# Layer 0's squared interactions as four tiles of 128 rows, two of 117 and a stacked half tile, in place of seven tiles of 117

## The reference

```python
z = einsum('bhd,bkd,hks->bsd', x0, xk, W) + b[None, :, None]
z = relu(z)
# layers 0 and 1: the first 64 maps are the next layer's xk, the other 64 go to the output
# layer 2: all 128 maps go to the output
```

## Time and profile before

| | |
|---|---|
| median of the runs | 2503.74 us (3 runs, 2494.42 to 2505.49) |
| the profiled execution | 2490.02 us, its span 2488.2 us |
| granted TensorE clock, mean over the span | 0.996 |
| PE, DVE, POOL, ACT busy | 96%, 90%, 67%, 43% |
| q1, the queue of the large DMAs | 461.35 MB, busy 76.7% of 16 engines |

### The profile page before, as it was taken

The page is one execution under the profiler, slowest core; times in us unless marked ns, Lnnn a source line. Parts: engine busy times, 40 slices in busy tenths (PEclk is TensorE's granted clock), DMA queues, the critical chain, the costliest instruction groups (busy, mean ns, idle before and its releaser), DMA issues. The chain is left out here.

```text
span 2488.2 us, 29429 instructions
## 1 busy us (share of the span) xinstructions
PE 2399.6 (96%) x7702; PEld 1442.7 (58%) x7702; DVE 2240.9 (90%) x1657; ACT 1058.4 (43%) x1053; POOL 1679.1 (67%) x1059
## 2 busy tenths in 40 slices
PE   0899999999999999999999999999999999999989
PEld 0465555665565666556556655656665555665556
DVE  0799998999999999999999999999999998999993
ACT  0244443444444444444444444443444443444445
POOL 7877766767677676777767677776768767544340
PEclk9999999999999999999999999999999999999999
DMA  6888787998778789888779887888988777888730
GB/s 162 203 197 196 193 191 183 208 215 191 190 199 191 196 212 213 189 190 199 191 196 216 207 190 187 201 192 197 215 210 188 192 197 173 210 205 195 182 79 11
DMA packets 172546, 469.79 MB, mean 189 GB/s; under 512 B 28987, under 2 KB 63163, under 8 KB 172245
## 3 DMA queue, kind: packets, MB, share of 16 engines
q1 hardware_dynamic: 148869, 461.35, 76.7%
q0 software_dynamic: 19968, 5.15, 2.2%
q10 hardware_dynamic: 3680, 2.95, 0.5%
HBM read 457.02 MB, written 12.33 MB: 189 GB/s over the span
## 5 line engine op out<-in xcount | busy, mean ns | idle before, releaser
L638 POOL TENSOR_TENSOR low<-prod,high 128x1024 fp32r<-128x1024 f32 x384 | 945.9, 2473 | 553.7 <-ACT high L801 551.2
L914 DVE TENSOR_TENSOR prod<-spread,maps 128x2048 f32<-128x2048 f32 x448 | 1016.7, 2281 | 72.8 <-ACT direct L743 20.9
L801 ACT ACTIVATE high<-prod 128x1024 fp32r<-128x1024 f32 (+1 forms) x576 | 596.2, 1056 | 715.9 <-DVE prod L914 458.4
L616 POOL DMA_INDIRECT landed<-in_tbl,rows_id x585 | 620.6, 1061 | 165.6 <-issue 148.6
L1014 PE MATMUL zacc_a<-prod,w_plain 128*128 128x512 f32 (+1 forms) x1536 | 709.1, 596 | 17.0 <-DVE prod L899 11.1
L1014 PE MATMUL zacc_b<-prod,w_plain 128*128 128x512 f32 (+1 forms) x1536 | 706.2, 594 | 5.9 <-DVE prod L914 5.9
L1014 PEld LDWEIGHTS zacc_a<-prod,w_plain 128*128 128x128 f32 (+1 forms) x1536 | 291.9, 190 | 288.9 <-issue 259.9
L1014 PEld LDWEIGHTS zacc_b<-prod,w_plain 128*128 128x128 f32 (+1 forms) x1536 | 291.2, 190 | 275.0 <-issue 246.8
L899 DVE TENSOR_TENSOR prod<-shifted,x_thrice 117x1024 f32<-117x1024 f32 x224 | 266.7, 1230 | 66.8 <-DMA shifted<-x_periods 53.7
L1049 PE MATMUL zacc_b<-low,w_high 128*128 128x512 f32 x672 | 281.2, 499 | 6.2 <-POOL low L638 6.2
L1049 PE MATMUL zacc_a<-low,w_high 128*128 128x512 f32 x672 | 280.7, 498 | 0.7 <-DVE low L869 0.5
(11 more groups left out here) (103 smaller groups left out, 1618.9 us busy)
## 6 DMA issues: line engine op xcount, KB each, us to landing
spread<-x_periods SPq DMA_DIRECT2D x608, 512.0 KB, 16.5
shifted<-x_periods SPq DMA_DIRECT2D x188, 468.0 KB
x_thrice<-x_periods SPq DMA_DIRECT2D x93, 156.0 KB
shifted<-x_periods SPq DMA_DIRECT2D x64, 156.0 KB
landed<-in_tbl,rows_id POOLq DMA_INDIRECT x585, 4.6
spread<-x_periods SPq DMA_DIRECT2D x32, 256.0 KB, 20.7
x_periods<-x SPq DMA_DIRECT2D x30, 256.0 KB, 2.2
spread<-features SPq DMA_DIRECT2D x4, 512.0 KB, 4.6
```

The lines of the kernel that those rows point to most:

```text
L616: nc.gpsimd.indirect_dma_start(out=landed[:, f, :], out_offset=None, in_=tables[f], in_offset=bass.IndirectOffsetOnAxis(ap=rows[:, f:f + 1 ...
L638: nc.gpsimd.tensor_tensor(low[0:rows, at_, :], prod[0:rows, at_, :], high[0:rows, slot(j, SPLIT, NH), :], ALU.subtract).then_inc(s_lowp, 1)
L801: nc.scalar.activation(high[0:rows, h, :], made(turn, j)[0:rows, :], ACT.Copy).then_inc(s_round, 1)
L914: nc.vector.tensor_tensor(prod[:, at_:at_ + 2, :], spread[:, t:t + 2, :], maps[:, :].unsqueeze(1).to_broadcast([128, 2, COLS]), ALU.mult). ...
```

## The change

Layer 0's 780 products are laid out anew. Tiles u = 0 to 3 get 11 more rows (117 to 127): fields 0 to 10 with the shifts 19, 18, 20, 21 (SPARE_SHIFTS). What is left for tile u = 6 is 40 rows (LAST_ROWS), which fit in half a tile: it becomes a stacked V tile of 64 rows. Its first operand is not x_thrice but a new buffer x_last. The weights are laid out to match (host side, laid_out).

- Each of u = 0 to 3 gets a second load of 11 rows (44 KB); x_thrice gets a fourth load of 11 rows; u = 6 is loaded by two DMAs of 20 rows (80 KB) in place of two of 39 rows, and x_last by two more of 20 rows, at the end of load_first. That makes 7 more DMAs a turn on SP's queue.
- Tile 26 is V: ACT makes its high part, DVE its low part (after the product of tiles 29 and 30), PE contracts it with four fp32r matmuls at tile 28 in place of four fp32 instructions at tile 26. At tile 26 PE does nothing; the count of s_mm for it is added at tile 25 (silent).
- ACT's take of layer 0 waits for PE's tile 28 and moves from tile 29 to tile 30 of its list.
- In the prologue load_thrice0 and load_shifted0 issue the extra rows too (one DMA with part 0, four with part 1), and load_last follows them. DVE clears half of x_last once.

```diff
+assert SHIFTS == PER0 * (N0 - 1) + 2
+SPARE = ROWS - TRIPLE
+SPARE_SHIFTS = (19, 18, 20, 21)
+LAST_RUN, LAST_GAPS = 10, ((19, 11, 20), (18, 11, 21))
+LAST_ROWS = 4 * LAST_RUN
...
-PLAN = "FVFPPPFPFFDPFDVFFPFV" "FFFFFFF" "FPFFFVPFDPVFDPPDFPFV"
+PLAN = "FVFPPPFPFFDPFDVFFPFV" "FFFFFFV" "FPFFFVPFDPVFDPPDFPFV"
-RELU0_AT, RELU1_AT, RELU2_AT = N1 + N0 - 1 + 3, N1 - 1 + 2, 3
+RELU0_AT, RELU1_AT, RELU2_AT = N1 + N0 - 1 + 4, N1 - 1 + 2, 3
...
 def rows_of(j):
     if j in SQUARED:
-        return TRIPLE
+        return HALF if j == SQUARED[-1] else ROWS if j - N1 < len(SPARE_SHIFTS) else TRIPLE
     t = j if j in PAIRED else j - N1 - N0
     return HALF * min(2, FIELDS - 2 * t)
-def shifts_of(u):
-
-    return min(PER0, SHIFTS - PER0 * u)
+def loads_of(u):
+
+    return 4 if u == N0 - 1 else 2 if u < len(SPARE_SHIFTS) else 1
+
+
+def last_pairs():
+
+    taken = {min((r, (r + e) % FIELDS), ((r + e) % FIELDS, r)) for r in range(SPARE) for e in SPARE_SHIFTS}
+    for n, (shift, first, gap) in enumerate(LAST_GAPS):
+        for t in range(LAST_RUN):
+            for b in range(2):
+                f = first + gap * b + t
+                g = (f + shift) % FIELDS
+                once = f < FIELDS and min((f, g), (g, f)) not in taken
+                yield 2 * LAST_RUN * n + 2 * t + b, f % FIELDS, g, once
 def stacked(j):
...
-                nc.sbuf_tensor("x_thrice_r", [TRIPLE, COLS], f32r) as x_thrice_r:
+                nc.sbuf_tensor("x_thrice_r", [ROWS, COLS], f32r) as x_thrice_r:
-        shifted = sb("shifted", [TRIPLE, RING0, COLS])
-        x_thrice = sb("x_thrice", [TRIPLE, COLS])
+        shifted = sb("shifted", [ROWS, RING0, COLS])
+        x_thrice = sb("x_thrice", [ROWS, COLS])
+        x_last = sb("x_last", [HALF, COLS])
...
         def load_thrice0(engine, part):
+            if part == 0:
+                engine.dma_start(x_thrice[TRIPLE:ROWS, :], chunk0(0, SPARE)).then_inc(s_thrice, 16)
             for s in range(PER0):
                 for lo, hi in runs_of(FIELDS - s, part):
                     engine.dma_start(x_thrice[s + PER0 * lo:s + PER0 * (hi - 1) + 1:PER0, :], chunk0(FIELDS - s + lo, hi - lo)
...
         def load_shifted0(engine, u, part):
+            if part == 1:
+                engine.dma_start(shifted[TRIPLE:ROWS, u, :], chunk0(SPARE_SHIFTS[u], SPARE)).then_inc(s_shifted[u], 16)
             for lo, hi in runs_of(PER0 * u, part):
                 engine.dma_start(shifted[PER0 * lo:PER0 * hi, u, :], chunk0(PER0 * u + lo, hi - lo).unsqueeze(1)
                                  .to_broadcast([hi - lo, PER0, COLS])).then_inc(s_shifted[u], 16)
...
+            def load_last(n, to, second):
+
+                for i, (shift, first, gap) in enumerate(LAST_GAPS):
+                    rows = period(n, first + (shift if second else 0), 2 * gap).rearrange("(b t) c -> t b c", b=2)
+                    sp.dma_start(to[2 * LAST_RUN * i:2 * LAST_RUN * (i + 1), :], rows[0:LAST_RUN, :, :]
+                                 ).then_inc(s_shifted[N0 - 1], 16)
+
             def load_shifted(n, u):
-                if shifts_of(u) == PER0:
-                    sp.dma_start(shifted[:, u % RING0, :], period(n, PER0 * u, FIELDS).unsqueeze(1).to_broadcast(
-                        [FIELDS, PER0, COLS])).then_inc(s_shifted[u], 16)
+                if u == N0 - 1:
+                    load_last(n, shifted[:, u % RING0, :], True)
                     return
-                for s in range(shifts_of(u)):
-                    sp.dma_start(shifted[s:TRIPLE - PER0 + s + 1:PER0, u % RING0, :], period(n, PER0 * u, FIELDS)
+                sp.dma_start(shifted[0:TRIPLE, u % RING0, :], period(n, PER0 * u, FIELDS).unsqueeze(1).to_broadcast(
+                    [FIELDS, PER0, COLS])).then_inc(s_shifted[u], 16)
+                if u < len(SPARE_SHIFTS):
+                    sp.dma_start(shifted[TRIPLE:ROWS, u % RING0, :], period(n, SPARE_SHIFTS[u], SPARE)
                                  ).then_inc(s_shifted[u], 16)
             def load_first(n):
...
                 for s in range(PER0):
                     sp.dma_start(x_thrice[s:TRIPLE - PER0 + s + 1:PER0, :], period(n, FIELDS - s, FIELDS)
                                  ).then_inc(s_thrice, 16)
+                sp.dma_start(x_thrice[TRIPLE:ROWS, :], period(n, 0, SPARE)).then_inc(s_thrice, 16)
                 for u in range(RING0):
                     load_shifted(n, u)
+                load_last(n, x_last, False)
             def load_spread(n, q):
                 for h in range(2):
...
+            sp.wait_ge(s_zero, 1)
+            load_last(Turn(None, 0), x_last, False)
...
+            nc.vector.memset(x_last[HALF // 2:HALF, :], 0.0).then_inc(s_zero, 1)
...
                     if u == 0 and turn.fixed and turn.number() == -1:
                         dve.wait_ge(s_prep, 3 if PARTED0 else 2)
                     if u == 0:
-                        dve.wait_ge(s_thrice, nxt.count(16 * PER0, 16 * PER0 + EXTRA_THRICE))
-                    loads = 1 if shifts_of(u) == PER0 else shifts_of(u)
+                        dve.wait_ge(s_thrice, nxt.count(16 * PER0 + 16, 16 * PER0 + 16 + EXTRA_THRICE))
+                    loads = loads_of(u)
                     dve.wait_ge(s_shifted[u], nxt.count(16 * loads, 16 * loads + EXTRA_SHIFTED[u]))
-                    nc.vector.tensor_tensor(to, shifted[0:rows, u % RING0, :], x_thrice[0:rows, :],
+                    nc.vector.tensor_tensor(to, shifted[0:rows, u % RING0, :], (x_last if u == N0 - 1 else x_thrice)[0:rows, :],
                                             ALU.mult).then_inc(s_square, 1)
                     return
                 t = j if j in PAIRED else j - N1 - N0
...
+            def silent(j):
+
+                return j < TILES and stacked(j) and PLAN[j - LATE] not in SPLIT
+
...
                     then = step_back(turn, j, LATE)
                     if then and PLAN[then[1]] in SPLIT:
                         done = contract_low(*then)
-                    done.then_inc(s_mm, 1)
+                    if not silent(j):
+                        done.then_inc(s_mm, 2 if silent(j + 1) else 1)
                 if turn.fixed and (turn.number(), j) in (
                         (-1, SQUARED[-1]), (CHUNKS - 1, PAIRED[-1]), (CHUNKS - 1, TILES - 1)):
```

More of the change, by code:

```diff
@@ L247, in build @@
         x = sb("x", [128, TURNED, ROWS])
-        with nc.sbuf_tensor("shifted_r", [TRIPLE, RING0, COLS], f32r) as shifted_r, \
-                nc.sbuf_tensor("x_thrice_r", [TRIPLE, COLS], f32r) as x_thrice_r:
-            pass
-        shifted = sb("shifted", [TRIPLE, RING0, COLS])
-        x_thrice = sb("x_thrice", [TRIPLE, COLS])
+        with nc.sbuf_tensor("shifted_r", [ROWS, RING0, COLS], f32r) as shifted_r, \
+                nc.sbuf_tensor("x_thrice_r", [ROWS, COLS], f32r) as x_thrice_r:
+            pass
+        shifted = sb("shifted", [ROWS, RING0, COLS])
+        x_thrice = sb("x_thrice", [ROWS, COLS])
+        x_last = sb("x_last", [HALF, COLS])
         direct01 = sb("direct01", [128, COLS])
@@ L286, in build @@
         s_thrice = sem("s_thrice")
+        s_zero = sem("s_zero")
         s_shifted = [sem(f"s_shifted{u}") for u in range(N0)]
@@ L709, in _ @@
                 act.wait_ge(s_prep, 1)
-                nc.scalar.activation(w_high[0:TRIPLE, parts12:plan_r, :], parts_in[0:TRIPLE, parts12:plan_r, :], ACT.Copy
+                nc.scalar.activation(w_high[:, parts12:plan_r, :], parts_in[:, parts12:plan_r, :], ACT.Copy
                                      ).then_inc(s_cast, 1)
@@ L852, in _ @@
             if PARTED0:
-                squares = parts_in[0:TRIPLE, parts12:plan_r, :]
+                squares = parts_in[:, parts12:plan_r, :]
                 done = nc.vector.tensor_tensor(squares, squares, w0_other[:, PLAIN0:N0, :], ALU.add)
@@ L860, in _ @@
                 dve.wait_ge(s_cast, 2)
[L861 to L862 removed]
+                nc.vector.tensor_tensor(w_low[:, parts12:plan_r, :], parts_in[:, parts12:plan_r, :],
+                                        w_high[:, parts12:plan_r, :], ALU.subtract).then_inc(s_prep, 1)
             def low_part(turn, j):
@@ L1164, in tile @@
         return np.concatenate([rows, rows]) if stacked(j) else rows
-    ab, ba = np.zeros((TRIPLE, N0, MAPS), np.float32), np.zeros((TRIPLE, N0, MAPS), np.float32)
+    ab, ba = np.zeros((ROWS, N0, MAPS), np.float32), np.zeros((ROWS, N0, MAPS), np.float32)
     for n, j in enumerate(SQUARED_ORDER):
         u, i = j - N1, np.arange(FIELDS)
-        for s in range(shifts_of(u)):
+        if u == N0 - 1:
+            for row, f, g, once in last_pairs():
+                if once:
+                    ab[row::HALF, n], ba[row::HALF, n] = w0[f, g], w0[g, f]
+            continue
+        for s in range(PER0):
             f, g = (i - s) % FIELDS, (i + PER0 * u) % FIELDS
-            ab[s::PER0, n] = w0[f, g]
+            ab[s:TRIPLE:PER0, n] = w0[f, g]
             if (u, s) != (0, 0):
-                ba[s::PER0, n] = w0[g, f]
+                ba[s:TRIPLE:PER0, n] = w0[g, f]
```

(4 more changed lines are left out.)

10 lines of the change are left out of this document (4 added, 6 removed).

## The result

The kernel after takes **2535.56 us** (median of 4 runs, 2532.56 to 2538.02) against 2503.70 for the kernel before (4 runs): ratio 1.013, 95% interval 1.0109 to 1.0151, or 31.9 us more. The forecast was 2515, 10.7 us of working on top of before. The sign and the place are as forecast; the size is three times as large. Of the signs that the forecast named, two turns take 146.65 us and not 145.6, and PE's busy time is 14.7 us less and not 24 us.

The account below looks back on a forecast made before the run. PE was taken to set the pace at 72.7 us a turn. New wait 3.7, late turns 4.3 and prologue 2.7 gave +10.7 us on the 2503.7 median, 2514.4, rounded to 2515 us; range 2496 to 2540.

Parts of the forecast that it names:

- the signs that the forecast named: Checks in the profile, among them two turns about 145.6 us apart and PE's busy time down some 24 us.
- PE's part: Tile 26 on PE: 0.78 us a turn less, 24 us over 31 turns if nothing waits; 128 rows cost nothing.
- The new wait: PE idles 0.8 us for tile 26's low part from DVE; tile 29 starts 0.12 us later, +3.7 us in all.
- Late turns: Late product of tile 27, formerly hidden, now delays PE: 1.9 us in turns 2 to 30, 2.4 in the last, +4.3.
- DVE's list: One more DVE instruction, 1.13 us a turn, absorbed by its waits for PE after tile 30: costed at nothing.
- The tight 0.7 us of ACT's tile 32: ACT's high part of tile 32 ready at S + 20.2, wanted by PE at S + 20.9: tight, costs nothing.
- Prologue: Before the turns: extra small loads on SP 1.6 us, plus layer 0's end at 4.2 us for 3.1; together +2.7 us.
- The sum: Whole kernel: 3.7 + 4.3 + 2.7 = +10.7 us, carried over to the median, 2515 us.
- The first: Rival, chance 0.15: tile 26's low part comes before PE wants it, 0.78 us a turn stay, 2482 us.
- The second: Rival, chance 0.17: added first loads delay the loads of u = 4 and 5; 2530 or 2545 us.
- The third, the clock: Rival, chance 0.03: a 0.8 us stall each turn lowers PE's clock, 1.7 us each, +52 us, 2567 us.
- the 0.70 us row: Profile row before the change: after 0.70 us idle, PE's pairs ran at once at 2.4 GHz's stride; cited against the clock rival.

Follow-up runs that it names:

- pool_waits: Kernel after, with POOL's low part of tile 28 made to wait for DVE's low part of tile 26: 2550.21 us, ratio 1.0181.
- before_again: Kernel before, unchanged, second repeat execution, with turn 0 starting at 134.3 us: 2504.88 us.
- low_between: Kernel after, with DVE's low part of tile 26 behind product 27/28 and the first sum step, the other steps a group later: 2514.34 us, ratio 1.0043.
- sums_late: Kernel after, with tile 26's low part directly behind product 27/28 and all three sum steps two groups later: 2522.05 us, ratio 1.0084.
- early_low: Kernel after, with DVE's low part of tile 26 right behind product 27/28, ahead of the sums: 2574.26 us, ratio 1.0328.
- after_relief: Kernel after, with layer 2's tile 32 in plain fp32, tile 26's low part left behind the sums: 2519.07 us, ratio 1.0111.
- again_before: Kernel before, unchanged, first repeat execution, with turn 0 starting at 119.6 us: 2493.96 us.
- before_relief: Kernel before, with only layer 2's tile 32 in plain fp32: 2493.25 us, ratio 1.0013.
- no_spare: Kernel after without the 11-row loads, those tiles at 117 rows and 44 products left out, tile 26 still split: 2517.02 us, ratio 1.011.
- full_plain: Kernel after, with tile 26 as a plain fp32 tile of 128 rows, 94 with zero weights, instead of split: 2505.79 us, ratio 1.0003.
- again_after: Kernel after, unchanged, run once more: 2533.67 us, ratio 1.013.

## Why the prediction was wrong

**PE's part** held: tile 27 at S + 11.22, and no cost of 128 rows.

**The new wait** was in its place, behind the instruction and of the kind that was worked out. The step that failed is "takes 1.22 to 1.25 us, the length of the same instruction for tile 19": it took 1.42 to 1.50, because POOL's low part of tile 28 was running when it began and not when tile 19's did. So a turn got 0.45 and 0.54 us longer, not 0.12: 14.9 us over the 30 turns from turn 0's start to turn 30's, for 3.6. Of the 0.33 us missing in an even turn 0.20 are this length; 0.10 are that the low part began at S + 13.52, 0.03 us behind the product, and not at S + 13.42, where line 936 began. pool_waits takes the collision away: it has the worked-out 0.8 us, and its even turns are 0.23 us longer than those of before. It could have been read beforehand. In the trace of before line 929 takes 0.42 us for 256 columns and line 936 0.65 for 128, with this beside it on POOL:

```profile
1010.59 0.42 DVE L929 TENSOR_TENSOR direct<-direct 128x256 f32<-128x256 f32 x1
```

```profile
1011.27 2.36 POOL L638 TENSOR_TENSOR low<-prod,high 128x1024 fp32r<-128x1024 f32 x1 [1.10 <-ACT high L801]
```

The same step takes 0.29 us in after, with POOL done. I took a delayed instruction's start for a free slot, and never laid POOL's timeline beside DVE's.

**Late turns** were costed at 4.3 us: 2.4 for the last turn, 1.9 for all others. The last turn came as worked out: its product is at S + 10.38, and what lies behind turn 30's start is 2.0 us longer. The 1.9 us came to 12.1 in the 30 turns in front of it. Of these the loads of u = 4 and 5 have 2.4, near what was costed: in turns 9, 13, 17, 19, 21 and 23 VectorE gets them so late that product 27/28 waits for them and not for the take. In turn 23 (S = 1839.44) it starts at S + 8.62, behind this wait:

```profile
1845.75 1.24 DVE L935 TENSOR_TENSOR prod<-shifted,x_thrice 117x1024 f32<-117x1024 f32 x1 [2.38 <-DMA shifted<-x_periods]
```

What the term lacked is the collision. Turn 1 alone has 6.2 us, from the 7.91 us low part and the clock behind it. Turn 15 has 1.9: its low part of tile 26 took 2.86 us, which makes PE's wait 1.37 us longer than in other odd turns, and the clock adds 1.7 (below), while before_again loses 1.1 us in that turn too. The rest was not followed: -1.1 in turn 0, 0.5 in turns 20 and 24, and 1.0 and 1.4 in turns 3 and 26, whose lengths differ by 0.9 and 2.9 us among the executions of before.

**DVE's list** was costed at nothing. That is a bound which the wait at tile 26 covered, and low_between uncovered it: VectorE, 1.13 us longer and without a pause from S + 8 on, takes back 0.6 us in an even and 0.9 in an odd turn. The tight 0.7 us of ACT's tile 32 cost nothing there; in sums_late, where the take comes later, they are the wait.

**Prologue**: 2.7 us forecast. Where turn 0 starts early, it starts at 121.3 and 121.0 us with the change's prologue (early_low, after_relief) and at 119.6 and 119.5 without (again_before, before_relief), one execution each: 1.4 to 1.8 us. Among the late starts the scatter, 130 to 136 us, hides it.

**The sum** of after against before_again, profile against profile: 1.6 in front of turn 0, 14.9 and 12.1 in the turns, 2.0 behind turn 30's start, 30.6 us; the medians say 31.9.

**The rivals.** The first fell, since a wait is there in every turn. The second fell with no_spare and full_plain. The third, the clock, did not come in the regular turns: behind stops of 0.95 to 1.78 us at tile 26 it stayed at 1.00. But it came in single turns of after. Around turn 1's 6.28 us wait and behind turn 15's wait of 2.43 us the granted clock was:

```profile
256.00:292.00 36.00, 29.72 (x96) 18.87 (x95) 33.18 (x22) 11.05 (x12) 18.30 (x11) 0.91 0.68 176
...
1262.00:1274.00 12.00, 9.57 (x25) 4.93 (x23) 11.81 (x10) 6.15 (x6) 7.30 (x6) 0.86 0.99 216
```

These are means of the levels 1.2 and 2.4 GHz. again_after has the same wait of 2.4 us in turn 15 without the fall, and the turn takes 74.97 us there and 76.63 in after: 1.7 us, the price that the rival named. after_relief has three such turns (19, 21, 23: a wait of 1.87 us, then 0.86 over 12 us, 76.7 us for 73.9), and early_low, with a wait of 2.0 us or more in nearly every turn, has some with the fall and more without. In turns 3 and 26 the clock falls behind POOL's low part in the kernel before too. So for stops of 1 us the 0.70 us row was the better guide than the rule of the Trainium skill ("TensorE: Matmul & The Clock Gate", section "A second HAM failure mode: psum-queue depth-cycling"), with which the regular turns do not agree; where the fall begins to come, these runs do not say. What was missing is a rival in which the duration of the late instruction itself is not what its rows elsewhere say.

## What to carry to other kernels

Work that is taken off the bounding engine is only worth what the next chain can follow. Here 0.78 us a turn on TensorE needed two more edits, one of VectorE's order and one of its amount of work, and with either alone the kernel stayed slower than before. When an instruction moves to a new place, take its duration from the rows of its new neighbours, not of its old ones: a subtraction of two SBUF operands on VectorE has one length by itself and another when a subtraction of GpSimd is running. And where an edit uncovers a chain, repeat the profile after mending the first wait; the second one was nearly of the same size. Look at GpSimd again after each edit: two of the mends tried here (early_low, pool_waits) moved the collision to another instruction and made it longer.

## What the runs showed of the hardware

- VectorE and GpSimd exclude each other when both run tensor_tensor with both sources in SBUF. VectorE's instruction that begins second ends 0.15 to 1.1 us behind GpSimd's and is shown as busy all the while: 1.42 us for 1.22, 2.88 for 0.68, 2.25 for 0.29, 7.91 for 1.22. It goes the other way too: GpSimd's 2.4 us instruction took 3.46 in before, where a subtraction of VectorE began with it. VectorE's instructions with one source in PSUM are untouched.
- A weight load that changes from 117 rows to 64, or from 64 to 128, is not hidden behind the matmul before it: 0.10 us more for each of two matmuls at each change, 0.38 us for one tile of 64 rows.
- The same kernel starts its turns at 119.6 us in one execution and at 134.3 in another. 12 of the 15 us lie in front of ScalarE's first take (97.38 for 82.27), and what holds it was not tried.
- TensorE's granted clock stayed at 1.00 with a stop of 1 us in every turn. It was 0.91 over the 36 us around a stop of 6.3, and behind a stop of 2.4 us it was 0.86 over 12 us in one execution (after) and did not fall in another (again_after); the fall cost 1.7 us.
